# Row maxima of attention scores read two PSUM banks at a time in the second layer

## The reference

```python
q = _split_heads(_lin(hidden_states, Wq, bq))
k = _split_heads(_lin(hidden_states, Wk, bk))
v = _split_heads(_lin(hidden_states, Wv, bv))
scores = jnp.einsum('bhsd,bhtd->bhst', q, k) * SCALE
attn = jax.nn.softmax(scores, axis=-1)
ctx = jnp.einsum('bhst,bhtd->bhsd', attn, v)
output = _lin(_merge_heads(ctx), Wo, bo)
rq = _split_heads(_lin(output, Wrq, brq))
rk = _split_heads(_lin(past_states, Wrk, brk))
rv = _split_heads(_lin(past_states, Wrv, brv))
rscores = jnp.einsum('bhsd,pbhtd->pbhst', rq, rk) * SCALE
rattn = jax.nn.softmax(rscores, axis=-1)
rctx = jnp.einsum('pbhst,pbhtd->pbhsd', rattn, rv)
```

## Time and profile before

| what | value |
|---|---|
| runs | 979.1, 990.27, 992.69 us; median 990.27 |
| span of the profiled execution | 1011.8 us |
| PE, DVE, ACT busy | 902.8, 755.7, 588.4 us |
| share of the chain that ended last | PE 61%, DVE 26% |
| reductions of the second layer | 512, busy 161.5 + 160.9 us |
| mean granted clock of TensorE | 0.93 of full |

### The profile page before, as it was taken

One profiled execution on the slowest core, in us unless ns is written; L12 is line 12 of the kernel. 1 busy time (PEld: TensorE's weight loads), 2 busy tenths in 40 slices (PEclk: granted clock), 3 DMA queues, 4 the chain that ended last, 5 costly groups with the idle time before them and its releaser, 6 DMA issues.

```text
span 1011.8 us, 17578 instructions
## 1 busy us (share of the span) xinstructions
PE 902.8 (89%) x6082; PEld 550.9 (54%) x6082; DVE 755.7 (75%) x2094; ACT 588.4 (58%) x1292; POOL 263.2 (26%) x400
## 2 busy tenths in 40 slices
PE   7799999878787989999999998998989999899991
PEld 6456665545677744443334233433334447889981
DVE  6888889876465768889897889889877635756673
ACT  2466666646564247887888687876666344333330
POOL 6123334364113353132100110010151030110263
PEclk9999999989999979999999699999798558999996
DMA  4336300010121100000000000004310001121122
GB/s 127 96 97 192 84 22 22 17 37 22 41 76 48 32 16 1 1 1 2 1 1 2 1 1 1 1 1 162 94 37 1 1 31 58 35 64 44 37 80 65
DMA packets 53040, 41.77 MB, mean 41 GB/s; under 512 B 5590, under 2 KB 44886, under 8 KB 52952
## 3 DMA queue, kind: packets, MB, share of 16 engines
q1 hardware_dynamic: 38504, 29.04, 9.8%
q0 software_dynamic: 3072, 6.30, 2.1%
q10 hardware_dynamic: 11376, 5.32, 1.8%
HBM read 22.55 MB, written 14.16 MB: 36 GB/s over the span
## 4 chain that ended last, share of the span: by engine, by line
PE 61%; DVE 26%; issue 4%; ACT 4%; POOL 2%; DVEq 1%; DMA 1%; another core or an unknown queue 0%; POOLq 0%; ACTq 0%
PE pv L1482 14%; PE ring L1445 9%; PE st L1460 8%; PE ring L1349 7%; DVE M L1769 5%; PE ring L1583 5%; DVE M L1776 4%; PE st L1570 4%; DVE ring L1773 3%; PE ring L1360 2%; PE ring L1407 2%; PE pv L1576 2%; ACT Et L1223 2%; PE st L1576 2%; PE st L1369 1%
## 5 line engine op out<-in xcount | busy, mean ns | idle before, releaser
L1223 ACT ACTIVATE Et<-st 128x512 f32<-128x512 f32 (+3 forms) x768 | 376.4, 550 | 166.7 <-PE st L1460 161.4
L1776 DVE TENSOR_REDUCE M<-ring 128x1 f32<-128x512 f32 x256 | 161.5, 684 | 36.1 <-PE ring L1445 32.6
L1769 DVE TENSOR_REDUCE M<-ring 128x2 f32<-128x512 f32 x256 | 160.9, 682 | 29.3 <-PE ring L1445 28.0
L1773 DVE CUSTOM_DVE_ANT_0 ring<-ring,maskw 128x128 f32<-128x128 f32 (+3 forms) x256 | 121.8, 511 | 24.5 <-PE ring L1445 23.0
L1482 PE MATMUL pv<-Et,Va 128*32 128x512 f32 (+3 forms) x1024 | 124.9, 543 | 1.6 <-POOL Et L1063 1.6
L1349 PE MATMUL ring<-ident,QK 128*128 128x128 f32 x512 | 85.9, 294 | 17.3 <-DVE M L1769 8.7
L1445 PE MATMUL ring<-Kbd,Qa 128*128 128x128 f32 (+3 forms) x256 | 89.7, 372 | 11.0 <-DVE M L1773 7.9
L1063 POOL TENSOR_SCALAR_AFFINE_SELECT Et<-Et 128x256 f32<-128x256 f32 x128 | 54.8, 430 | 138.8 <-ACT Et L1223 137.3
L1445 PE MATMUL ring<-RKT,Qa 32*128 32x512 f32 x256 | 83.5, 537 | 8.2 <-DVE M L1769 6.2
L1460 PE MATMUL st<-Qb,Kbd 128*128 128x512 f32 (+3 forms) x256 | 85.2, 353 | 3.9 <-ACT Et L1223 3.8
L1482 PE MATMUL pv<-Et,RV 128*32 128x512 f32 x512 | 83.8, 720 | 0.0
(11 more groups left out here) (245 smaller groups left out, 1457.1 us busy)
## 6 DMA issues: line engine op xcount, KB each, us to landing
Yd<-Yt ACTq DMA_DIRECT2D x76, 64.0 KB
Xs<-Xd SPq DMA_DIRECT2D x16, 256.0 KB, 3.0
L1W<-in_L1W SPq DMA_DIRECT2D x2, 2048.0 KB, 12.1
Kbd<-Ksb SPq DMA_DIRECT2D x60, 64.0 KB, 2.0
Xd<-zero SPq DMA_DIRECT2D x6, 512.0 KB, 3.7
W<-in_L0W SPq DMA_DIRECT2D x8, 258.0 KB, 4.0
W<-in_L0W SPq DMA_DIRECT2D x8, 256.0 KB, 4.4
Xd<-zero SPq DMA_DIRECT2D x4, 448.0 KB, 4.6
```

The lines of the kernel that those rows point to most:

```text
L1223: e.activation(Et[s // 2 % 4][:, j % 2, q0:512], st[s % NST][:, q0:512], ACT.Exp, scale=SCALE).then_inc(exp_done, 1)
L1769: e.tensor_reduce(M[i][:, t, j, :], bank(ph)[:, :].rearrange("p (two n) -> p two n", two=2), AX.X, ALU.max).then_inc(mx_red, 1)
L1773: e.tensor_tensor_reduce(bank(ph)[:, 0:n], bank(ph)[:, 0:n], maskw[:, 512 - n:512], 1.0, -3e38, ALU.add, ALU.max, M[i][:, t, j, 0:1]).then ...
L1776: e.tensor_reduce(M[i][:, t, j, 0:1], bank(ph)[:, 0:n], AX.X, ALU.max).then_inc(mx_red, 1)
```

## The change

The four ring banks become one PSUM tensor `rings`, of which `ring[i]` are slices, at the same places. In the second layer, the two `mx` of a step (j and j + 1) always take consecutive banks of the ring. Where the first of them is bank 0, 1 or 2 the two lie side by side, and DVE waits for both matmuls, takes both maxima (self) or all four (rec) with one reduction over 1024 elements, and adds 2 to `mx_red`. Where the pair is banks 3 and 0, there are two reductions as before. PE's, ACT's and POOL's instructions and their order stay.

```diff
@@ -524,7 +524,8 @@
         pv = ps("pv", 512)
-        ring = [ps(f"ring{i}", 512) for i in range(NRING)]
+        rings = ps("rings", 512 * NRING)
+        ring = [rings[:, 512 * i:512 * i + 512] for i in range(NRING)]
         st = [ps(f"st{i}", 512) for i in range(NST)]
@@ -1764,6 +1765,20 @@
                     n = 128 * (t + 1) if l == 0 else 512
                     if t == 0 and j == (0, 2)[l] and n_mcol["mcol", l, u] >= 2:
                         dve.wait_ge(mcol_done, n_mcol["mcol", l, u] - 1)
+                    mate = n_ring.get(("mx", l, u, t, j - 1)) if l == 1 and j % 2 else None
+                    if mate is not None and mate % NRING < NRING - 1:
+                        continue
+                    if l == 1 and j % 2 == 0 and n_ring[ph] % NRING < NRING - 1:
+                        r0 = 512 * (n_ring[ph] % NRING)
+                        two = rings[:, r0:r0 + 1024]
+                        dve.wait_ge(mx_full, m + 2)
+                        if kind == "rec":
+                            e.tensor_reduce(M[i][:, t, j:j + 2, :], two.rearrange("p (j past n) -> p j past n", j=2, past=2),
+                                            AX.X, ALU.max).then_inc(mx_red, 2)
+                        else:
+                            e.tensor_reduce(M[i][:, t, j:j + 2, 0], two.rearrange("p (j n) -> p j n", j=2),
+                                            AX.X, ALU.max).then_inc(mx_red, 2)
+                        continue
                     dve.wait_ge(mx_full, m + 1)
```

## The result

The changed kernel takes 1018.2 us (median of 4 runs, 1013.43 to 1020.6), the kernel before 989.56 beside it (979.1 to 992.69). The ratio is 1.038 with a 95% interval of 1.0335 to 1.0424. A second comparison, made with the experiments, gave 1012.25 us against 992.32 and 1.026 (1.0201 to 1.0326). By the ratios the change costs 38 and 26 us, by the differences of the medians 29 and 20.

A forecast was written before the change was run, and what follows sets the result against it. PE and DVE were taken to bound the kernel by waiting on each other in a four-bank ring. Terms +27.7 + 3 − 1.5 − 3 − 2 gave +24 us on 990, at 0.98: 1014 us, range 995 to 1033.

The forecast's parts named there:

- The bound: Layer 2 ring: PE and DVE wait on each other; a pair's first reduction releases the next pair's second matmul.
- The merged instruction: On DVE: one 1024-element reduction lasts 1.21 us, saves 0.07 us a pair, 13 us (9 to 16) over 193 pairs.
- Rival D: Merged instruction not cheaper per element, for instance 1.36 us: DVE saves nothing, ties cost 0.68, +35 us, 1024; chance 0.04.
- The step: Layer 2 step with one other bank between pairs, the first pair merged: period 3.34 us against 2.82.
- The number of ties: 52 layer 2 matmuls start within 0.06 us of a to-be-merged pair's first reduction ending; 0.53 us each, 27.7 us.
- The sum: Whole kernel, profiled execution: +27.7 + 3 − 1.5 − 3 − 2 = +24 us; ends of unknown terms +8 and +40.
- the wait for the second matmul: DVE's merged reduction waits for both matmuls of its pair; said to cost nothing, as they run side by side.
- the places with a cushion: 24 layer 2 places with 0.06 to 0.6 us to spare; late by 5.4 us together, taken as 3.
- The transpositions tied to a first reduction: PE's ring transposes (L1349), 21 places, nearly all at unit starts: put at 0, 11 us if each stood alone.
- Rival A: DVE is the bound, so its shorter line goes straight to the end: 13 us less, 977 us; chance 0.10.
- Rival B: Delay mostly absorbed by later waits both kernels share: half the sum, +8 to +15, 1002 us; chance 0.15.
- Rival C: TensorE's clock falls more often: six more 17 us stretches give 1032, all 69 such steps 1064; chance 0.14.

The follow-up runs named there:

- the other 124 pairs: Kernel before with common tensor, merging only the 124 pairs without exactly one other ring fill before the next pair: ratio 0.997, on repeat 1.0104.
- the 69 pairs: Kernel before with common tensor, merging only the 69 pairs with exactly one other ring fill before the next pair: ratio 1.019 (1.0137 to 1.0242).

## Why the prediction was right, point by point

*The bound.* The tie of a pair's second matmul to the first reduction of the pair ahead was read rightly as the critical handover. Holding the bank without merging reproduces most of the loss (14.6 of 15.8 us in the clean units), and merging away from the ties costs far less (0.4).

*The merged instruction.* 1.21 us was forecast, 1.22 measured, 193 of them. Rival D (1.36 us) is out. The saving on DVE's line was summed to 13 us (9 to 16) and is 7; the estimate by the Trainium skill's page (VectorE: DVE Perf Modes, Side-by-side: where the cycles go for N=2048 bf16) was 30. It is not on the path, so the sum doesn't feel it. The idle time was to rise to over 90 and is 90.2.

*The step.* 3.34 forecast, 3.33 measured, but so close only because two errors cancel. The terms were 0.53 + 1.21 + 0.06 + 0.50 + 1.04; the timeline has 0.63 + 1.22 + 0.06 + 0.43 + 0.99. The reduction starts 0.10 us later than before, a term that was put at nothing, and the two stretches behind the tied matmul got 0.12 shorter. Where those stretches were already short, the 0.10 shows: over the 31 ties in the clean units the step grew by 0.61 us in the median, not by 0.53.

*The number of ties.* 31 of the 52 lie in the clean units; at 0.53 they make 16.5 us, and with their real growth, delays that were swallowed included, 16.2. Measured for all that the change does there are 15.8. *The sum,* +24 us on the profile, compares with 20 and 29 in the medians, 26 and 38 by the ratios and 24.6 at equal time at half clock; 1014 was forecast and 1018.2 came. That the last agrees so well is partly luck, with a tie that cost more than its 0.53.

*Terms put too low.* Merging the other 124 pairs as well costs 1.5 us over the clean units beyond the 69 (0.4 when they are merged alone). Most of it is in two places. Unit 9 takes 13.17 us for 12.60. There DVE starts on the last merged pair at 477.55, 0.60 us after the pair's second matmul, which was late (in the trace of the 69 pairs, where this pair is not merged, DVE had started 0.14 us before that matmul); its next work, the normalization `xh` (L1720), so ends at 479.79, and PE idles 0.46 us for it before the transposition at 479.94. The prediction had put at nothing both the wait for the second matmul and what is queued behind the merged instruction; by this timeline both cost here. The wait alone, without merging, costs unit 9 only 0.13 us (11.98 for 11.85). Without merging, with both banks held (193 pairs), unit 9 takes 12.67, so the release alone doesn't do it either. Unit 6 takes 16.21 us for 15.57; a pair at 439.22 waits 0.36 us for a merged reduction, one of the places with a cushion (0.26 us in the trace of before). The transpositions tied to a first reduction were put at nothing because a delay isn't paid twice, and that holds where I followed it: in unit 14 one starts 0.53 us later than in the trace of the 69 pairs, and the second matmul of the next pair starts no later than there.

*Rival A* (DVE is the bound) is out: its line did get shorter and the time longer. *Rival B* (delays absorbed) is out for the clean units, where the sum of the ties arrived nearly whole. *Rival C* (the clock falls more often) is not what costs: in the second comparison the executions of both kernels had half the clock for 120 us on average. Nor do these rows show it, first before and then after, 340 to 800 us, with the granted clock third from the end:

```profile
340.00:800.00 460.00, 424.63 (x2730) 188.93 (x2728) 381.36 (x783) 328.36 (x643) 96.29 (x128) 0.93 0.06 19
```

```profile
340.00:800.00 460.00, 415.81 (x2636) 179.59 (x2635) 362.24 (x563) 322.76 (x627) 95.88 (x127) 0.93 0.06 19
505.87:509.20 3.33, 2.95 (x24) 1.13 (x20) 2.44 (x3) 3.09 (x7) 0.00 (x0) 1.00 0.00 0
```

The prediction's share of 2.6 of 3.34 us for PE in the new step was too low: the row gives 2.95 of 3.33, since the first matmul of the pair runs for 0.49 of the 0.87 us between the two. That layer 1 and the experts would be unchanged can't be checked on these two profiles: the stage behind the attention, which the change doesn't touch, is 12.6 us shorter in the second. The gaps in PE's work of the kind that the Trainium skill names (TensorE: Matmul & The Clock Gate, A second HAM failure mode: psum-queue depth-cycling) are in this trace, 0.38 us by the row at 507.78, and the clock stayed at 2.4 GHz through that step.

## What to carry to other kernels

Where two engines hand buffers to each other in a ring, look for the buffer whose release starts the next piece of work. Merging two instructions saves only what does not already overlap (here 0.07 us where they queue and 0.04 on average, not the 0.15 that one duration suggests). It gives the first buffer back later by what the instruction has grown (0.53 us), and the merged instruction starts later too (0.10 us here, of which 0.03 to 0.04 are the wait for both matmuls). It pays only where the next user of the first buffer has that much time to spare, and that can be counted in the trace of before, place by place. Moving the work that makes the tie may only tie it to another engine.

## What the runs showed that I had not expected

TensorE's granted clock differs between executions of equal work by more than most edits are worth. The kernel that waits for both matmuls, whose full-clock units are those of the kernel before, had a ratio of 0.987 in one comparison and 1.000 in another, each with an interval that excludes the other value, and the 124 merges had 0.997 and 1.010. Set against the time at half clock, the four come to between −0.2 and +3.6 us. A kernel's two profiles can fall into the same places (the change's units all but one agree within 0.1 us between its two profiles, half-clock units included), so more runs of one kernel need not average it out. Chips differ as well: at 125 and 120 us at half clock the kernel before takes 1006 us on one chip and 989 on another. Below 1.5% I would trust only stretches at equal clock, or times set against the time at half clock, as in the table.
